# Gram-Schmidt inside an attention kernel: vectors as rows of 64 partitions instead of columns, the leading row spread by DMA

## The chip, the cores and the metric

The kernel runs on one core of a Trainium2 chip. A core has five engines that run side by side, each through its own queue of instructions in strict order: TensorE (PE in the profile, with PEld for its weight loads), VectorE (DVE), ScalarE (ACT), GpSimd (POOL) and SyncE (SP, which here only issues DMAs). They meet only at semaphores. The metric is the device time of one execution in microseconds.

## What is computed

An attention block with a bias, a feed-forward block, and a response whose matrices come from two orthonormalised 256 x 32 matrices U and V. Cut to what matters here:

```python
def gram_schmidt(X):                       # X is 256 x 32
    for i in range(32):
        q = Q[:, i]
        q = q / (norm(q) + EPS)
        Q = Q.at[:, i].set(q)
        coeffs = q @ Q[:, i + 1:]
        Q = Q.at[:, i + 1:].add(-outer(q, coeffs))
...
scores = q @ k.T / 4 + attention_bias      # 32 batches, 16 heads, 256 x 256
scores = where(src_mask, -inf, scores)
probs = softmax(scores)
x = x + (probs @ v) @ Wo + bo
x = x + gelu2(ln(x) @ W1 + b1) @ W2 + b2
...
U_o = gram_schmidt(U); V_o = gram_schmidt(V)
basis = U_o @ V_o.T
response = ((x @ basis) @ basis.T[:, :32]) @ resp_w.T + resp_b + safety_bias
out = x + strength * response
```

Gram-Schmidt has 32 steps, each dependent on the one before. There are also 32 batches, and the kernel does one step in each batch of the attention.

## The kernel before

It has two stages. The first loops over the 32 batches of the attention and stores the result x2 to DRAM; the second loops over them again for the feed-forward block and the response. `run_batches` writes out the first three and last three batches and loops over the rest, two at a time. Each engine has a `body` that is written by hand: what stands in it is what the engine does in one period, in that order, and several batches are in flight at once (the tail of batch b-1, the main part of b, the preparation of b+1).

The parts of a period that matter here, by engine:

- **PE**: `scores` (four heads at a time, L1185), `transposes` of the exponentials (one head at a time, four 128x128 transposes, L1200), `pv` (L1223), the projections, `project_o` (L1287). `transposes(b, h)` writes one of two PSUM banks, so it waits until head h-2 has been copied out of that bank. Heads 3, 7 and 11 are copied by DVE (`copy_pT`, L607), the others by ACT (L922). Head 13 therefore waits for DVE's copy of head 11.
- **DVE**: `reduce_head` (L601, two instructions of 256 columns for each head, each with a short read of its accumulator), copies out of PSUM, statistics of a later batch (`stats`, L501).
- **ACT**: the exponentials (L917) and most copies.
- **POOL**: it adds the mask to the bias of four heads at a time, `add_mask` (L430, two instructions of 1024 columns each, both operands in SBUF), makes the mask's values (L420) and normalises x (L397 to L411).
- **SP**: it loads bias, x and mask, and stores x2. The bias of half a batch is two transfers of 1 MB (L288).

A Gram-Schmidt step goes round all of them. U and V lie as columns, 128 partitions by 2 x 2 x 32 (`uv`). ACT copies out column i (`gs_column`, L938). PE multiplies it, spread over 128 columns, with all the vectors, and so gets its products with each in every partition (`gs_gram`, L1159, four matmuls of 32 columns, between `ctx_transpose` and the transposes of head 10). DVE takes the squared norm and masks the products to later vectors (`gs_products`, L577 and L579, behind head 15 and ahead of `stats` and the copy of head 11). POOL, one period on, takes the root and adds epsilon (`gs_norm`, L376 and L379), DVE inverts it (`gs_reciprocal`, L583), ACT scales (`gs_coefficients`, L943 and L944), POOL forms four outer products and adds them (`gs_update`, L386 and L389), and ACT writes the finished column back (`gs_write`, L950).

After the last batch `response_matrix` makes the matrices of the second stage from U and V.

Of the kernel before, what the change touches and what calls it, by code (L numbers as in the profile page):

```python
# [31 lines left out]
P = 128  # L32
# [81 lines left out]
def attention_block_kernel(nc, x, itok, fside, score, mask, W_ada, b_ada, Wq, bq, Wk, bk, Wv, bv, Wo, bo,  # L114
                           W1, b1, W2, b2, g2, beta2, U, V, safety_bias, gate_w1T, gate_b1, gate_w2T, gate_b2,
                           resp_wT, resp_b, freqs, out):
    with ExitStack() as ctx:
# [6 lines left out]

        x2_d = nc.dram_tensor("x2_d", (B, S, D), F32, kind="Internal").ap()
# [7 lines left out]
        ident = sb("ident", [P, P]); later = sb("later", [P, R, R]); expo = sb("expo", [P, 2, 2])  # L133
# [6 lines left out]
        uv = sb("uv", [P, 2, DC, R]); ucol = sb("ucol", [P, 2, DC]); gsb = sb("gsb", [P, 2, R]); gii = sb("gii", [P, 2])  # L140
        nrm = sb("nrm", [P, 2]); nrme = sb("nrme", [P, 2]); rnrm = sb("rnrm", [P, 2]); qcol = sb("qcol", [P, 2, DC]); gprod = sb("gprod", [P, 2, DC, R]); coef = sb("coef", [P, 2, R])
# [71 lines left out]
        gs_ps = bank[7][:, 0:2 * R].rearrange("p (a r) -> p a r", a=2)  # L213
# [4 lines left out]
        s_gcol = sem("s_gcol"); s_gram = sem("s_gram"); s_gii = sem("s_gii"); s_gnrm = sem("s_gnrm"); s_gp = sem("s_gp"); s_grec = sem("s_grec"); s_gcoef = sem("s_gcoef"); s_gprod = sem("s_gprod"); s_gupd = sem("s_gupd"); s_gself = sem("s_gself")  # L218
# [20 lines left out]
        def load_x01(sp, i):  # L239
# [5 lines left out]
                     (uv[:, 0], columns(U)), (uv[:, 1], columns(V))]  # L245
# [25 lines left out]
        def _(sp):  # L271
# [87 lines left out]
        def _(pool):  # L359

            nc.gpsimd.memset(ident[:], 0.0)
            nc.gpsimd.memset(later[:], 1.0)
# [5 lines left out]
            nc.gpsimd.affine_select(out=later[:], in_=later[:], compare_op=ALU.is_gt, fill=0.0, base=0,  # L368
                                    pattern=[[-1, R], [1, R]], channel_multiplier=0).then_inc(s_const, 1)
# [65 lines left out]
            def body(b, n):  # L435
# [52 lines left out]
        def _(dve):  # L488
# [43 lines left out]
            ins.then_inc(s_perm, 1)  # L532
            nc.vector.memset(half[:, 0:1], 0.0)
# [37 lines left out]

            def gs_products(b):
                i = b.n
                dve.wait_ge(s_gram, i + 1)
                if b.i is not None or b.off >= 1:
                    dve.wait_ge(s_gcoef, i)
                nc.vector.tensor_copy(gii[:], gs_ps[:, :, bass.ds(i, 1)].rearrange("p a r -> p (a r)"))  # L577
                ahead = later[:, bass.ds(i, 1)].to_broadcast([P, 2, R])
                nc.vector.scalar_tensor_tensor(gsb[:], gs_ps, -1.0, ahead, ALU.mult, ALU.mult).then_inc(s_gii, 1)  # L579
# [5 lines left out]
            def response_matrix():  # L585

                dve.wait_ge(s_rm, 1)
# [926 lines left out]
```

## Time and profile before

| | us |
|---|---|
| median of three runs | 1352.67 (1352.37 to 1352.85) |
| the profiled execution | 1352.78 |
| its span in the trace | 1350.6 |
| busy: PE, PEld | 1302.0, 1101.9 |
| busy: DVE, ACT, POOL | 1071.7, 1084.2, 871.8 |

The first stage takes the span up to about 885 us, the second the rest. Share of busy time is read by stage: POOL works over nine tenths of the first stage and about a quarter of the second. The time between the span and the profiled execution's own time, about 2.2 us, lies around the program.

### The profile page before, as it was taken

To read this page: it belongs to the slowest core of one execution; us is meant where nothing else is said; L and a number is where in the kernel's file an instruction comes from. 1 tells how busy PE (TensorE), PEld (TensorE's weight loads), DVE (VectorE), ACT (ScalarE), POOL (GpSimd) and SP (SyncE) were. 2 spreads that over 40 slices of the span, in tenths; PEclk is the share of its full clock that TensorE was granted. 3 is DMA by queue.
4 is the path that set the end of the run, shared out by engine and by line. 5 is a ranking of instruction groups with operands and counts; after the bars stand their busy time and mean duration, and the time that the engine had idled before them with its cause. 6 is when DMAs were issued, how large, how long until landed. Compare 5 with 4: busy or idle time off the path is not lost. (4 is left out here: it accounts for less than half of the span.)

```text
span 1350.6 us, 39501 instructions
## 1 busy us (share of the span) xinstructions
PE 1302.0 (96%) x11802; PEld 1101.9 (82%) x11802; DVE 1071.7 (79%) x3669; ACT 1084.2 (80%) x2697; POOL 871.8 (65%) x874
## 2 busy tenths in 40 slices
PE   4999999999999999999999999879999999999997
PEld 3777777777777777777777777559999999999996
DVE  4777787877778787777878778668888888888885
ACT  1788888888888888888888887867888888888873
POOL 4999989998998999899999989322222222222210
PEclk9999999999999999999999999979999999999998
DMA  9646555564655556465555674010101111111100
GB/s 288 191 146 211 174 183 181 173 210 146 211 169 186 178 175 205 150 211 166 190 174 179 203 224 133 25 32 25 47 31 47 31 46 31 39 38 34 43 25 32
DMA packets 182669, 175.05 MB, mean 130 GB/s; under 512 B 15552, under 2 KB 182112, under 8 KB 182624
## 3 DMA queue, kind: packets, MB, share of 16 engines
q1 hardware_dynamic: 181248, 173.64, 40.4%
q10 hardware_dynamic: 1376, 0.85, 0.2%
q8 instruction: 24, 0.39, 0.1%
q14 instruction: 21, 0.17, 0.0%
HBM read 157.69 MB, written 16.78 MB: 129 GB/s over the span
## 5 line engine op out<-in xcount | busy, mean ns | idle before, releaser
L430 POOL TENSOR_TENSOR ring<-ring,maskv 128x1024 f32<-128x1024 f32 x256 | 600.0, 2371 | 12.2 <-DMA ring<-in_fside 4.9
L917 ACT ACTIVATE ring<-ring,nmax 128x256 f32<-128x256 f32 x1024 | 452.6, 502 | 24.1 <-DVE nmax L601 24.1
L601 DVE CUSTOM_DVE_ANT_0 ring<-bank,ring 128x256 f32<-128x256 f32 x1024 | 373.1, 419 | 90.5 <-PE bank L1185 72.9
L922 ACT ACTIVATE pT<-bank 128x512 f32<-128x512 f32 x416 | 239.3, 592 | 102.0 <-PE bank L1200 101.9
L1200 PE MATMUL bank<-ident,ring 128*128 128x128 f32 x2048 | 292.3, 278 | 1.4 <-ACT pT L922 1.1
L1200 PEld LDWEIGHTS bank<-ident,ring 128*128 128x128 f32 x2048 | 231.7, 142 | 70.8 <-issue 47.9
L1052 ACT ACTIVATE work<-bank,b1t 128x256 f32<-128x256 f32 x256 | 107.6, 476 | 76.0 <-PE bank L1394 76.0
L1185 PE MATMUL bank<-work 32*128 32x256 f32 x2048 | 148.5, 404 | 6.0 <-DVE nmax L601 5.2
L1394 PE MATMUL bank<-hT_high,w_high 128*128 128x256 f32 x512 | 148.0, 289 | 4.3 <-DVE hT_rest L774 2.4
L1407 PE MATMUL bank<-w_high,gT_high 128*128 128x256 f32 x512 | 148.0, 289 | 0.0
L1394 PE MATMUL bank<-hT_rest,w_high 128*128 128x256 f32 x512 | 145.5, 284 | 0.0
L1407 PE MATMUL bank<-w_high,gT_rest 128*128 128x256 f32 x512 | 145.2, 284 | 0.0
L1407 PE MATMUL bank<-w_rest,gT_high 128*128 128x256 f32 x512 | 145.2, 284 | 0.0
L1394 PE MATMUL bank<-hT_high,w_rest 128*128 128x256 f32 x512 | 145.1, 283 | 0.0
L1223 PE MATMUL bank<-pT,vt 128*32 128x256 f32 x2048 | 137.0, 385 | 2.7 <-ACT pv_sb L928 1.6
L462 POOL TENSOR_SCALAR vpeb<-mvb 128x2 f32<-128x2 f32 x32 | 6.2, 194 | 201.6 <-DVE mvb L690 201.4
L1185 PEld LDWEIGHTS bank<-work 32*128 32x128 f32 x2048 | 93.4, 186 | 38.3 <-issue 27.8
L476 POOL TENSOR_TENSOR work<-work,b2b 128x512 f32<-128x512 f32 x32 | 41.7, 1302 | 126.2 <-DVE work L805 126.2
L790 DVE SCALAR_TENSOR_TENSOR pT<-work 128x512 f32<-128x512 f32 x128 | 88.6, 692 | 42.2 <-ACT work L1056 29.8
L1394 PEld LDWEIGHTS bank<-hT_high,w_high 128*128 128x128 f32 x512 | 97.8, 191 | 4.9 <-DVE hT_rest L774 2.6
L1407 PEld LDWEIGHTS bank<-w_rest,gT_high 128*128 128x128 f32 x512 | 98.5, 192 | 0.0
L1407 PEld LDWEIGHTS bank<-w_high,gT_high 128*128 128x128 f32 x512 | 98.4, 192 | 0.0
(161 smaller groups left out, 2666.8 us busy)
## 6 DMA issues: line engine op xcount, KB each, us to landing
ring<-in_fside SPq DMA_DIRECT2D x128, 1024.0 KB, 7.6
xt<-in_x SPq DMA_DIRECT2D x32, 256.0 KB, 3.1
x_d<-x2s SPq DMA_DIRECT2D x32, 256.0 KB, 7.9
work<-x_d SPq DMA_DIRECT2D x32, 256.0 KB, 2.7
out<-pT SPq DMA_DIRECT2D x32, 256.0 KB, 2.2
mk<-in_mask SPq DMA_DIRECT2D x32, 64.0 KB, 6.7
w<-in_W SPq DMA_DIRECT2D x2, 1024.0 KB, 10.5
wada<-in_W_ada SPq DMA_DIRECT2D x1, 512.0 KB, 8.1
```

Source lines behind the costliest of these rows:

```text
L430: nc.gpsimd.tensor_tensor(v, v, m, ALU.add).then_inc(s_masked, 1)
L476: nc.gpsimd.tensor_tensor(yb[:, b.par], y2[:, b.par], b2b[:].unsqueeze(1).to_broadcast([P, QT, D]), ALU.add).then_inc(s2_yb, 1)
L601: nc.vector.tensor_tensor_reduce(out=v, in0=score_ps[h % HG][:, qt], in1=v, scale=-1.0, scalar=ROW_MAX_NEG, op0=ALU.add, op1=ALU.min, accu ...
L790: nc.vector.scalar_tensor_tensor(gT[:, 2 * j:2 * j + 2], th[:, j], 1.0, up[:, j], ALU.add, ALU.mult).then_inc(s2_g, 1)
L917: nc.scalar.activation(v, v, ACT.Exp, bias=nmax[:, b.par, h, qt:qt + 1], scale=-1.0).then_inc(s_exp, 1)
L922: nc.scalar.activation(pT[:, h % (2 * HG)], tp_ps[h % 2], ACT.Copy).then_inc(s_pta, 1)
L1052: ins = nc.scalar.activation(th[:, j, f], tiles2(j)[:, f], ACT.Tanh, bias=b1t[:, 2 * j + f:2 * j + f + 1], scale=0.5 * GELU_A)
L1185: ins = mm(score_ps[r][:, qt], qm[rows, b.par, a, c, qt * P:(qt + 1) * P], kT[rows, b.par, c], start=True, stop=True)
L1200: ins = nc.tensor.transpose(tp_ps[h % 2][:, kt, qt * P:(qt + 1) * P], ring[:, slot, qt, h % CH, kt * P:(kt + 1) * P], ident[:])
L1223: ins = mm(pv_ps[VW * j:VW * (j + 1), :], vt[:, b.par, kt, h], pT[:, h % (2 * HG), kt], start=(kt == 0), stop=(kt == QT - 1))
L1394: ins = mm(tiles2(j)[:, f], w1s[kw][:, c, n * P:(n + 1) * P], hTs[kx][:, b.par, c], start=(c == 0 and k == 0), stop=(c == DC - 1 and k == ...
L1407: ins = mm(tiles2(4)[:, t], gTs[kx][:, b.par, f, t * P:(t + 1) * P], w2s[kw][:, f], start=(f == 0 and k == 0), stop=(f == FC - 1 and k == ...
```

## The change

The vectors of U and V are now kept as rows: `uvT` has 64 partitions (32 vectors of U, then 32 of V) of 256 columns. A step is done on all 64 at once.

- At the start PE transposes the columns (`vectors_transposed`) and DVE copies them to `uvT` (`gs_start`).
- In each period SP waits for the update of the step before, writes `uvT` to DRAM, waits for that, and loads row i of U and row i of V, each spread over 32 partitions, into `row`. This stands behind the mask's load and ahead of the bias transfer of batch b+2 (`vector_rows`).
- `gs_gram`, `gs_column` and `gs_write` are gone. DVE forms the products of every vector with the leading one, and its squared norm, as two sums along 256 columns (`gs_products`), with `uvT` and `row` both in SBUF.
- Which vector is earlier, leading or later is a column of a table (`roles`), that ACT copies out (`gs_role`). `gs_coefficients` is three instructions of one column, each waiting for the one before.
- POOL's `gs_norm` also scales `uvT` by a role (`uvz`), and `gs_update` is one product and one sum of 64x256. `gs_update` moves from behind `add_mask(b, 3)` to ahead of it.
- After the last batch PE transposes the rows back, and the response's matrices take one step more; DVE's copies for it stand behind its `split_weights(0)`.

```diff
+            def vector_rows(b):
+                sp.wait_ge(s_gupd, b.n + 1)
+                sp.dma_start(uv_d, uvT[:]).then_inc(s_uvst, 16)
+                sp.wait_ge(s_uvst, 16 * b.n + 16)
+                for a in range(2):
+                    sp.dma_start(row[a * R:(a + 1) * R], uv_d[bass.ds(b.n + a * R, 1)].rearrange("o d -> (o d)").partition_broadcast(R)).then_inc(s_row, 16)
...
                     load_mask(b.plus(2))
+                vector_rows(b)
                 if n is None or n + 2 < B:
                     sp.wait_ge(s_tp, H * b.n + CH)
                     load_bias(b.plus(2), 0)
...
             def gs_norm(i):
                 pool.wait_ge(s_gii, i + 1)
+                pool.wait_ge(s_grole, i + 1)
                 pool.nop(nofuse=True)
-                nc.gpsimd.tensor_tensor(nrm[:], gii[:], expo[:, 1], ALU.pow).then_inc(s_gp, 1)
+                nc.gpsimd.tensor_tensor(nrm[:], gii[:], expo[0:2 * R, 1, 0:1], ALU.pow).then_inc(s_gp, 1)
+                nc.gpsimd.tensor_scalar(uvz[:], uvT[:], role[:, 2:3], 1.0, ALU.mult, ALU.mult)
...
             def gs_update(i):
-                for a in range(2):
-                    for c in range(DC):
-                        ins = nc.gpsimd.tensor_scalar(gprod[:, a, c], coef[:, a], qcol[:, a, c:c + 1], 1.0, ALU.mult, ALU.mult)
-                ins.then_inc(s_gprod, 1)
+                nc.gpsimd.tensor_scalar(gprod[:], row[:], coef[:, 0:1], 1.0, ALU.mult, ALU.mult).then_inc(s_gprod, 1)
                 pool.wait_ge(s_gprod, i + 1)
-                nc.gpsimd.tensor_tensor(uv[:], uv[:], gprod[:], ALU.add).then_inc(s_gupd, 1)
+                nc.gpsimd.tensor_tensor(uvT[:], uvz[:], gprod[:], ALU.add).then_inc(s_gupd, 1)
...
                     add_mask(b, 2)
-                    add_mask(b, 3)
                 if step:
                     gs_update(b.plus(-1).n)
+                if main:
+                    add_mask(b, 3)
...
             def gs_products(b):
-                dve.wait_ge(s_gram, i + 1)
+                dve.wait_ge(s_row, 32 * b.n + 32)
                 if b.i is not None or b.off >= 1:
                     dve.wait_ge(s_gcoef, b.n)
-                nc.vector.tensor_copy(gii[:], gs_ps[:, :, bass.ds(i, 1)].rearrange("p a r -> p (a r)"))
-                nc.vector.scalar_tensor_tensor(gsb[:], gs_ps, -1.0, ahead, ALU.mult, ALU.mult).then_inc(s_gii, 1)
+                nc.vector.scalar_tensor_tensor(prods[:, 0], uvT[:], 1.0, row[:], ALU.mult, ALU.mult, accum_out=dot[:])
+                nc.vector.scalar_tensor_tensor(prods[:, 1], row[:], 1.0, row[:], ALU.mult, ALU.mult, accum_out=gii[:]).then_inc(s_gii, 1)
...
             def gs_coefficients(i):
+                act.wait_ge(s_gii, i + 1)
+                act.wait_ge(s_grole, i + 1)
+                nc.scalar.activation(dotm[:], dot[:], ACT.Copy, scale=role[:, 0:1]).then_inc(s_gdot, 1)
                 act.wait_ge(s_grec, i + 1)
+                act.wait_ge(s_gdot, i + 1)
+                nc.scalar.activation(share[:], dotm[:], ACT.Identity, bias=role[:, 1:2], scale=rnrm[:, 0:1]).then_inc(s_gshare, 1)
+                act.wait_ge(s_gshare, i + 1)
+                nc.scalar.activation(coef[:], share[:], ACT.Copy, scale=rnrm[:, 0:1]).then_inc(s_gcoef, 1)
...
                 if main:
-                    gs_gram(b, n)
                     transposes(b, 10)
                     transposes(b, 11)
```

Where this stands in the engines' queues, taken from a batch that is written out. On DVE, at the end of a batch's heads, before (`gii` and `gsb` are the squared norm and the masked products, `pT` takes the copy of head 11, L601 is the reduction of a head):

```order
L601 ISA ring,nmax<-bank,ring 128x256
L601 ISA nmax 128x1
L577 COPY gii<-bank 128x2
L579 SCALAR_TENSOR_TENSOR gsb<-bank,later 128x64
L501 BN_STATS st<-xt 128x6 x2
L607 COPY pT<-bank 128x512
```

and of the change (L622 is the reduction now, L628 the copy of head 11):

```order
L622 ISA ring,nmax<-bank,ring 128x256
L622 ISA nmax 128x1
L596 SCALAR_TENSOR_TENSOR prods,dot<-uvT,row 64x256
L597 SCALAR_TENSOR_TENSOR prods,gii<-row 64x256
L512 BN_STATS st<-xt 128x6 x2
L628 COPY pT<-bank 128x512
```

Two instructions on PSUM are replaced by two of 256 columns whose inputs both lie in SBUF, still ahead of the copy of head 11.

On POOL, from one step's norm to the next batch's first mask additions, before (`ring` is the bias):

```order
L376 TENSOR_TENSOR nrm<-gii,expo 128x2
L379 TENSOR_SCALAR nrme<-nrm 128x2
L430 TENSOR_TENSOR ring<-ring,maskv 128x1024 x4
L386 TENSOR_SCALAR gprod<-coef,qcol 128x32 x4
L389 TENSOR_TENSOR uv<-uv,gprod 128x128
L420 TENSOR_SCALAR maskv<-mk 128x512
L430 TENSOR_TENSOR ring<-ring,maskv 128x1024 x2
L397 TENSOR_SCALAR vpe<-mv 128x2
```

and of the change (L440 is the mask addition now):

```order
L388 TENSOR_TENSOR nrm<-gii,expo 64x1
L389 TENSOR_SCALAR uvz<-uvT,role 64x256
L392 TENSOR_SCALAR nrme<-nrm 64x1
L440 TENSOR_TENSOR ring<-ring,maskv 128x1024 x2
L397 TENSOR_SCALAR gprod<-row,coef 64x256
L399 TENSOR_TENSOR uvT<-uvz,gprod 64x256
L440 TENSOR_TENSOR ring<-ring,maskv 128x1024 x2
L430 TENSOR_SCALAR maskv<-mk 128x512
L440 TENSOR_TENSOR ring<-ring,maskv 128x1024 x2
L407 TENSOR_SCALAR vpe<-mv 128x2
```

The update now has two mask additions more behind it and two fewer ahead of it.

## Rows read from the trace of the kernel before

**Rows 1.** Busy by stretch: us from:to, length, engines (instructions), PE clock, DMA.

```profile
400.00:500.00 100.00, 100.00 (x960) 77.14 (x962) 79.11 (x330) 85.43 (x214) 91.22 (x86) 1.00 0.57 183
```

**Rows 2.** Timeline of PE: start, length, line, operation, count [idle before].

```profile
417.08 1.15 PE L1185 MATMUL bank<-work 32*128 32x256 f32 x16
...
419.09 0.98 PE L1159 MATMUL bank<-uv,ucol 128*128 128x32 f32 x8
...
419.90 1.07 PE L1200 MATMUL bank<-ident,ring 128*128 128x128 f32 x8
...
421.91 1.15 PE L1185 MATMUL bank<-work 32*128 32x256 f32 x16
...
422.98 1.09 PE L1200 MATMUL bank<-ident,ring 128*128 128x128 f32 x8
```

**Rows 3.** Timeline of DVE, same period, and one reciprocal earlier.

```profile
404.88 0.16 DVE L583 RECIPROCAL rnrm<-nrme 128x2 f32<-128x2 f32 x1
...
418.50 0.43 DVE L601 CUSTOM_DVE_ANT_0 ring<-bank,ring 128x256 f32<-128x256 f32 x1 [0.99 <-PE bank L1185]
...
421.26 0.15 DVE L577 COPY gii<-bank 128x2 f32 x1
...
421.46 0.74 DVE L501 BATCH_NORM_STATS2 st<-xt 128x6 f32<-128x256 f32 x2
...
422.12 0.67 DVE L607 COPY pT<-bank 128x512 f32<-128x512 f32 x1
```

**Rows 4.** Timeline of ACT: the last of the four coefficient instructions.

```profile
410.32 0.31 ACT L944 ACTIVATE coef<-gsb,rnrm 128x32 f32<-128x32 f32 x1
```

**Rows 5.** Timeline of POOL over one period.

```profile
410.81 1.08 POOL L386 TENSOR_SCALAR gprod<-coef,qcol 128x32 f32<-128x32 f32 x4 [1.10 <-ACT coef L944]
411.96 0.46 POOL L389 TENSOR_TENSOR uv<-uv,gprod 128x128 f32<-128x128 f32 x1
...
413.30 4.69 POOL L430 TENSOR_TENSOR ring<-ring,maskv 128x1024 f32<-128x1024 f32 x2 [0.17 <-POOL maskv L420]
...
419.81 1.10 POOL L411 TENSOR_SCALAR xn<-xt,rstd,nmr 128x256 f32<-128x256 f32 x2 [0.21 <-POOL nmr L402]
...
425.51 0.72 POOL L376 TENSOR_TENSOR nrm<-gii,expo 128x2 f32<-128x2 f32 x1
...
426.67 9.35 POOL L430 TENSOR_TENSOR ring<-ring,maskv 128x1024 f32<-128x1024 f32 x4
437.10 1.07 POOL L386 TENSOR_SCALAR gprod<-coef,qcol 128x32 f32<-128x32 f32 x4 [1.08 <-ACT coef L944]
```

**Rows 6.** Timeline of DVE and POOL where both read SBUF at once.

```profile
841.90 2.59 DVE L675 TENSOR_TENSOR cb<-cb 128x256 f32<-128x256 f32 x1
...
902.45 0.68 DVE L798 TENSOR_TENSOR gT_rest<-pT,gT_high 128x512 fp32r<-128x512 f32 x1
903.05 1.75 DVE L774 TENSOR_TENSOR hT_rest<-work,hT_high 128x512 fp32r<-128x512 f32 x1
```

**Rows 7.** The same place on POOL.

```profile
902.54 1.71 POOL L476 TENSOR_TENSOR work<-work,b2b 128x512 f32<-128x512 f32 x1
```

**Rows 8.** One line's instructions: count, shortest/median/longest ns, first and last start.

```profile
L469 POOL TENSOR_TENSOR nmrb<-mnegb,rstdb x32: 196/672/737, 884.3 to 1296.0; 128x2 f32<-128x2 f32 x32
```

**Rows 9.** DMA issues: tensors, queue, count, KB each, median us to landing.

```profile
xt<-in_x SPq DMA_DIRECT2D x32, 256.0 KB, 3.1
x_d<-x2s SPq DMA_DIRECT2D x32, 256.0 KB, 7.9
```

**Rows 10.** Timeline of SP: the bias transfer behind the new place.

```profile
415.16 1.00 SPq L288 DMA_DIRECT2D ring<-in_fside  x2
```

**Rows 11.** Timeline of PE after idle times of two lengths.

```profile
865.00 1.07 PE L1223 MATMUL bank<-pT,vt 128*32 128x256 f32 x16 [1.17 <-DVE ctxn L649]
...
904.86 0.46 PE L1394 MATMUL bank<-hT_high,w_high 128*128 128x256 f32 x1 [2.37 <-DVE hT_rest L774]
```

**Rows 12.** Busy by stretch behind the second of them.

```profile
904.90:908.30 3.40, 3.40 (x16) 3.40 (x17) 3.19 (x6) 2.08 (x6) 0.00 (x0) 0.52 0.33 82
```

More of the change, by code:

```diff
@@ L361, in _ @@
             nc.gpsimd.memset(ident[:], 0.0)
-            nc.gpsimd.memset(later[:], 1.0)
+            nc.gpsimd.memset(tri[:], -1.0)
             nc.gpsimd.memset(expo[:, 0], -0.5)
@@ L367, in _ @@
                                     pattern=[[-1, P]], channel_multiplier=1)
-            nc.gpsimd.affine_select(out=later[:], in_=later[:], compare_op=ALU.is_gt, fill=0.0, base=0,
-                                    pattern=[[-1, R], [1, R]], channel_multiplier=0).then_inc(s_const, 1)
+            nc.gpsimd.affine_select(out=tri[:], in_=tri[:], compare_op=ALU.is_gt, fill=0.0, base=0,
+                                    pattern=[[-1, 2 * R]], channel_multiplier=1).then_inc(s_const, 1)
             pool.wait_ge(s_const, 1)
@@ L532, in _ @@
             ins.then_inc(s_perm, 1)
+            for a in range(2):
+                rows = slice(a * R, (a + 1) * R)
+                nc.vector.tensor_copy(roles[rows, 0], tri[rows, a * R:(a + 1) * R])
+                nc.vector.tensor_copy(roles[rows, 1], ident[rows, a * R:(a + 1) * R])
+                link(nc.vector.tensor_scalar(roles[rows, 2], ident[rows, a * R:(a + 1) * R], -1.0, 1.0, ALU.mult, ALU.add))
             nc.vector.memset(half[:, 0:1], 0.0)
@@ L757, in body @@
                 if n == B:
-                    response_matrix()
+                    response_matrix(0)
                     split_weights(0)
+                    response_matrix(1)
             reduces(first, (0, 1, 2))
+            gs_start()
             v_out(first)
@@ L1007, in body @@
                 if main:
-                    gs_column(b.n)
+                    gs_role(b.n)
                     copy_pT(b, 8)
@@ L1148, in bias_rows, with vectors_transposed @@
                 mm(bank[6][:, 0:2 * DC], perm[:], bqr[:].rearrange("p t c -> p (t c)"), start=True, stop=True).then_inc(s_bqk, 1)
-            def gs_gram(b, n):
-                pe.wait_ge(s_gcol, b.n + 1)
-                if n is None or n + 1 < B:
-                    pe.wait_ge(s_v, b.n + 2)
-                if n is None or n >= 1:
-                    pe.wait_ge(s_gself, b.n)
-                for a in range(2):
-                    for c in range(DC):
-                        ins = mm(gs_ps[:, a], ucol[:, a, c:c + 1].to_broadcast([P, P]), uv[:, a, c], start=(c == 0), stop=(c == DC - 1))
-                ins.then_inc(s_gram, 1)
+            def vectors_transposed():
+                for c in range(DC):
+                    ins = nc.tensor.transpose(bank[6][0:2 * R, c * P:(c + 1) * P], uv[:, c].rearrange("p a r -> p (a r)"), ident[:])
+                ins.then_inc(s_uvt, 1)
             def response_matrix(step):
                 if step == 0:
-                    pe.wait_ge(s_gself, R)
+                    pe.wait_ge(s_gupd, R + 1)
                     pe.wait_ge(s_reduced, 2 * H * B)
                     for c in range(DC):
-                        mm(bank[0][0:R, 0:R], uv[:, 1, c], uv[:, 1, c], start=(c == 0), stop=(c == DC - 1))
-                    ins = mm(bank[1][0:R, 0:D], uv[0:R, 0, 0], respT[:], start=True, stop=True)
+                        ins = nc.tensor.transpose(bank[2][:, 2 * R * c:2 * R * (c + 1)], uvT[:, c * P:(c + 1) * P], ident[0:2 * R, 0:2 * R])
                 if step == 1:
                     pe.wait_ge(s_rmc, 1)
+                    for c in range(DC):
+                        mm(bank[0][0:R, 0:R], uv[:, c, 1], uv[:, c, 1], start=(c == 0), stop=(c == DC - 1))
+                    ins = mm(bank[1][0:R, 0:D], uv[0:R, 0, 0], respT[:], start=True, stop=True)
+                if step == 2:
+                    pe.wait_ge(s_rmc, 2)
                     ins = mm(t_ps, gram[:].rearrange("p k r -> p (k r)"), t1[:], start=True, stop=True)
@@ L1209, in pv @@
                         pe.wait_ge(s_ctxn, 2 * b.n)
+                    else:
+                        pe.wait_ge(s_gupd, 1)
                 if g == 1:
@@ L1297, in _ @@
             pe.wait_ge(s_load_att, 16 * len(loads_att))
+            vectors_transposed()
             project_v(first)
-            x_back(first, False)
+            x_back(first)
             def y_transpose(b):
@@ L1366, in body @@
                     response_matrix(1)
+                    response_matrix(2)
                 if main:
```

60 lines of the change are left out of this document (25 added, 35 removed).

## The prediction, made before the change was run

> **What bounds the kernel now.** I read the slices and the busy times by stretch first: in the first stage PE is never idle and its clock is full, with POOL at 91% and ACT and DVE below that [rows 1]. Then PE's timeline: each group of matmuls begins about when the one before it ends, so a period is the sum of PE's work [rows 2]. The period is the distance between two updates on POOL, 437.10 - 410.81 = 26.29 us [rows 5]. The second stage is bound by PE too, and the change doesn't touch its loop. So the question is what happens to the 26.29 us in each of some 30 periods. The span lies 2.2 us under the execution's own time of 1352.78; the sum is made against 1352.78, which is 0.1 above the median.
>
> **What the change removes.** PE loses `gs_gram`: it starts at 419.09, and the next transposes at 419.90 [rows 2], so 0.81 us a period of the engine that sets the period, or 31 x 0.81 = 25 us in all if nothing else becomes late. ACT trades four coefficient instructions and a column's write for three chained ones of one column. The last of the four ends at 410.32 + 0.31 = 410.63 [rows 4], and I leave the end of the coefficients there; a few tenths either way do nothing below but shift POOL.
>
> **What it adds on DVE, and why that is on the path.** PE's transposes of head 13 wait for DVE's copy of head 11, since both use one PSUM bank. Heads 12 and 13 are the eight matmuls from 422.98; the second four begin half of 0.91 us later, at 423.44. DVE's copy ends at 422.12 + 0.67 = 422.79 [rows 3]. So the copy may come 0.65 us later before PE notices it at today's period. It can't come earlier: it stands behind the eight reductions from 418.50 [rows 3], and those stand behind PE's scores at 417.08 [rows 2], which are ahead of the removed matmuls. That makes a new loop: scores of heads 12 to 15, reductions, products, statistics, copy of head 11, transposes of head 13, the rest of PE's period. Its length is 26.29 + (delay of the copy - 0.65). Against it, PE's own work is 25.48.
>
> The copy is delayed by what the two products take over the 0.20 us that `gs_products` takes now (421.26 to 421.46, [rows 3]). The eight reductions ahead of them have 256 columns and an accumulator's read too, and take 421.26 - 418.50 = 2.76, which is 0.345 each from start to start [rows 3]. An undisturbed sum of 512 columns takes 0.68 [rows 6], so the products can't cost much more. I take 0.35 to 0.40 each; alone the pair takes 0.75, and the delay is 0.55: just inside the 0.65.
>
> **But they are not alone.** Both inputs of each product are in SBUF, and POOL's mask additions read SBUF nine tenths of the time. The trace has that meeting in other places. At 902.45 DVE runs such an instruction, POOL's addition issued at 902.54 takes 1.71 us until 904.25, and DVE's next, issued at 903.05, takes 1.75 us instead of 0.68: it stood until POOL was done [rows 6, 7]. So one waits for the other in full, and of two DVE instructions in a row the second is overtaken by POOL's waiting one. In the first stage itself the one sum of 256 columns of two SBUF tensors took 2.59 us, one mask addition longer than it should [rows 6]. In the second stage POOL's product of two columns takes 196 ns alone but 672 in the median, beside DVE's SBUF work [rows 8]. None of DVE's instructions in a period of the first stage has two SBUF inputs today: scores, copies and additions read one input from PSUM.
>
> The Trainium skill states this as a rule ("SBUF — State Buffer", section "Who interferes with whom"): a DVE instruction with two SBUF inputs and a GpSimd instruction that reads SBUF exclude each other, and the one that came second blocks until the first has ended. By that rule the change costs what the next part works out; without it the pair costs 0.75 us and the change about nothing. The rows on tensors of 128 partitions agree with it; none shows 64.
>
> **Which POOL instruction the products meet.** POOL's order decides, and the change moves it. The update begins 0.18 us behind the coefficients, at 410.81 [rows 4, 5]. Its product of 256 columns costs 0.55 (half of the 1.10 for two of that size), its sum 0.73: between 0.46 for 128 columns and 2.34 (4.69 / 2) for 1024, by the line through both [rows 5]. With gaps it ends at about 412.2. Then the two mask additions that used to be ahead of it, 4.69, to 416.95; the mask's values with the gaps around them, 413.30 - 411.96 - 0.46 = 0.88, to 417.8; the next batch's first two additions, 4.69, to 422.4 or 422.5 [rows 5]. DVE's products are due at 421.26 [rows 3]: inside the second addition, which runs from about 420.1. The first product then waits 1.15 us, to 422.4, and takes some 0.35. Next on POOL stands a small instruction (`vpe`, about 0.2), then the second product, 0.35. The statistics start at 423.3 instead of 421.46, a delay of 1.85, and the loop is longer by 1.85 - 0.65 = 1.2 us; with the coefficients 0.1 to 0.2 us earlier it is 1.05. I take **1.15 us a period**.
>
> **POOL keeps up.** Its period holds 1.1 us of waiting for the coefficients [rows 5], so 25.2 of work. It gains the scaling of `uvT` (0.55 and a gap), and the update changes from 1.54 to 1.28; that makes 25.6, and some tenths of waiting for DVE, under 27.4. Today it waits behind all four groups of masks, tomorrow behind three, so it runs a group later against DVE: the norm comes at about 422.5 + (425.51 - 413.30 - 4.69) = 430.0 in place of 425.51 and is done by 431.8, with the scaling between [rows 5]. DVE asks for it at 404.88 + 26.29 + 1.15 = 432.3 [rows 3]. The heads 12 to 15 get their mask at 416.95, DVE needs it at 418.50. Thin, but it fits.
>
> **SP and the transfers.** `uvT` goes out at 412.2, and the rows are needed at 421.26: 9 us for two transfers in a row. A transfer in a quiet queue lands in 3.1 us (x), one behind bias loads in 7.9 (x2) [rows 9]; here the bias of the next batch has been under way since 401 and is in, so I take 3.1 each, and with 1 us for issuing the rows are there by 419.5. The bias transfer of batch b+2, now issued at 415.16 [rows 10], goes out a little later, at about 416; POOL reads it a period on, so this costs nothing. The extra traffic is 64 KB out and 64 KB in a period, next to 2 MB of bias.
>
> **Ends of the program.** In the last two batches POOL has no more masks to add, so nothing meets; there the kernel gains a few tenths. The transposes and copies at the start and the longer `response_matrix` cost a few tenths each. I take +0.5 in all. Sum: 1352.78 + 30 x 1.15 + 0.5 = 1387.8, so **1388 us**. The case's own range is 1371 to 1403: a first product that waits 0.6 to 1.65 us.
>
> **Rivals.**
>
> *A. The products don't wait* (64 partitions, or this form, might not exclude POOL). Then the delay is 0.55 against 0.65, the loop is 26.19, and with the ends the time is 1352.78 - 30 x 0.1 + 0.5 = 1350. This is the side on which the change is not slower: it is faster once the pair costs under 0.83, and the most it could give, with free products, is 0.65 a period or 1333. For it: no row shows 64 partitions. Against: every row with two SBUF inputs beside POOL shows the wait.
>
> *B. POOL is later by over 1.2 us*, so that the products fall into the first of the two additions. The first product waits for its end, POOL takes its second addition, and the second product waits for all of it: 2.2 to 3.4 us a period, 1419 to 1455. For it: a slower update or late coefficients move POOL that way. Against: 1.2 us is as much as the whole update is priced at.
>
> *C. PE's clock falls in the new gap.* PE would be ready for head 13 at 422.6 to 423 and starts at 424.6, idle for 1.6 to 1.9 us. After 1.17 us idle matmuls ran on at full speed; after 2.37 us one took 0.46 [rows 11], and the granted clock of the 3.4 us behind it was 0.52, nearly all of it at the lower level of 1.2 GHz [rows 12]. The gap lies between. Half speed for 3.4 us costs 1.7: 30 x 2.85 + 0.5 gives 1439. With B it is 1470 to 1506.
>
> *D. The rows come late.* At 7.9 us for each transfer they come at 429, 7.8 us behind the products' place: over 200 us more. For it: the same queue carries the bias; against: the order of the issues.
>
> **How the numbers follow.** The forecast's case gets 0.60, A 0.12, B 0.12, C 0.10, D 0.06. Something under 0.2% (2.7 us) can't be told from no change. A lies at that bound, so I give faster 0.04, same 0.09; slower 0.87. The range that leaves out A, D and the upper part of B is **1358 to 1456**: it takes in a first product that hardly waits, and the clock's case.
>
> **What would show it.** Right: two products on DVE of which the first takes about 1.5 us and the second 0.6; PE idle ahead of a transpose group, released by DVE's copy of head 11; a period of 27.4 on POOL, whose wait for the coefficients is still there, about 1.5 us long. A: products of 0.4 us and a period of 26.2. B: a second product of 2.5 us or more. C: a granted clock under 1.00 in the first stage. D: DVE waiting for `row`. The forecast is wrong at its root if the copy of head 11 isn't what PE waits for.

## The result, and the profile after the change

| | before | after |
|---|---|---|
| median of four runs, us | 1352.76 (1352.37 to 1354.17) | 1390.80 (1385.48 to 1391.91) |
| the profiled execution, us | 1352.78 | 1385.48 |
| its span, us | 1350.6 | 1383.7 |

The changed kernel is slower: 1.0272 times the time before, 95% interval 1.0244 to 1.0299. The forecast was 1388. A second set of runs of the same kernel, `r_after` below, gave 1388.05 and 1.0265 (1.0244 to 1.0286), so I take the two together: 35 to 38 us more. Two of the ten executions of `b1_one_input` below (1376.01 and 7208.93 us) fell in a slower state of the chip and are left out of its figures; every other execution used here is a fast one.

First the two lines of the page after that say most: the busy times, and PE's transposes with the idle time ahead of them and what ended it.

```profile
PE 1288.7 (93%) x11550; PEld 1076.5 (78%) x11550; DVE 1120.6 (81%) x3741; ACT 1082.3 (78%) x2633; POOL 872.8 (63%) x810
...
L1215 PE MATMUL bank<-ident,ring 128*128 128x128 f32 x2048 | 300.9, 279 | 43.5 <-DVE pT L628 42.7
```

PE is busy 13 us less than before (1302.0). The matmuls that went (L1159) were busy for 31.3 us, in part overlapping their neighbours, and the transposes, in shorter groups now, are busy for 300.9 us instead of 292.3. PE stands idle for 42.7 us until DVE's copies into `pT` (L628) are done. The same kernel's busy times by stretch (length, engines, PE clock, DMA) show it in the steady state; before, PE was busy for all of these 100 us [rows 1].

```profile
400.00:500.00 100.00, 93.72 (x888) 70.73 (x889) 80.81 (x324) 82.20 (x197) 89.15 (x77) 1.00 0.57 177
```

PE's timeline of the changed kernel, around the end of one period and at the same place a period earlier (start, length, idle time before in brackets); it answers to [rows 2].

```profile
410.56 0.65 PE L1215 MATMUL bank<-ident,ring 128*128 128x128 f32 x4 [1.45 <-DVE pT L628]
...
430.51 1.15 PE L1200 MATMUL bank<-work 32*128 32x256 f32 x16
...
434.82 1.15 PE L1200 MATMUL bank<-work 32*128 32x256 f32 x16
435.90 0.66 PE L1215 MATMUL bank<-ident,ring 128*128 128x128 f32 x4
438.00 0.65 PE L1215 MATMUL bank<-ident,ring 128*128 128x128 f32 x4 [1.45 <-DVE pT L628]
```

The transposes of heads 12 and 13 used to run as one group of eight. Now head 12 runs at 435.90, PE then waits 1.45 us, and head 13 runs when the copy of head 11 has left its bank. The distance of two such waits is the new period: 438.00 - 410.56 = 27.44 us, against 26.29 before. 26 periods in a row have this wait, each 1.44 to 1.47 long.

What holds the copy back is on DVE, beside POOL (timelines of the changed kernel, same period; they answer to [rows 3] and [rows 5]):

```profile
434.68 0.08 DVE L622 DVE_READ_ACCUMULATOR2_ANT nmax<- 128x1 f32 x1
434.68 1.58 DVE L596 SCALAR_TENSOR_TENSOR prods<-uvT,row 64x256 f32<-64x256 f32 x1
...
436.19 0.41 DVE L597 SCALAR_TENSOR_TENSOR prods<-row 64x256 f32<-64x256 f32 x1
...
436.54 0.74 DVE L512 BATCH_NORM_STATS2 st<-xt 128x6 f32<-128x256 f32 x2
437.20 0.67 DVE L628 COPY pT<-bank 128x512 f32<-128x512 f32 x1
```

```profile
424.43 0.47 POOL L397 TENSOR_SCALAR gprod<-row,coef 64x256 f32<-64x256 f32 x1 [2.18 <-ACT coef L970]
424.98 0.72 POOL L399 TENSOR_TENSOR uvT<-uvz,gprod 64x256 f32<-64x256 f32 x1
425.67 4.67 POOL L440 TENSOR_TENSOR ring<-ring,maskv 128x1024 f32<-128x1024 f32 x2
...
431.29 4.68 POOL L440 TENSOR_TENSOR ring<-ring,maskv 128x1024 f32<-128x1024 f32 x2 [0.17 <-POOL maskv L430]
436.07 0.24 POOL L407 TENSOR_SCALAR vpe<-mv 128x2 f32<-128x2 f32 x1
```

The first product is issued at 434.68, inside POOL's mask addition, and ends at 436.26, 0.29 after the addition's end (435.97). The second stands beside POOL's short `vpe` and takes 0.41. In the last batch POOL has no masks left, and there the first product takes 0.41 too:

```profile
904.73 0.41 DVE L596 SCALAR_TENSOR_TENSOR prods<-uvT,row 64x256 f32<-64x256 f32 x1
```

### The profile page after: what moved, and what is told of

Its sections match the earlier page's. It is cut to its first block and busy times, and to the rows that moved or that the text cites. A ratio compares the mean times of both kernels' runs of the same rounds, so it can differ in the third digit from the quotient of the medians.

```text
span 1383.7 us, 39096 instructions
## 1 busy us (share of the span) xinstructions
PE 1288.7 (93%) x11550; PEld 1076.5 (78%) x11550; DVE 1120.6 (81%) x3741; ACT 1082.3 (78%) x2633; POOL 872.8 (63%) x810
## 5 line engine op out<-in xcount | busy, mean ns | idle before, releaser
L440 POOL TENSOR_TENSOR ring<-ring,maskv 128x1024 f32<-128x1024 f32 x256 | 601.0, 2369 | 12.1 <-DMA ring<-in_fside 4.7
L622 DVE CUSTOM_DVE_ANT_0 ring<-bank,ring 128x256 f32<-128x256 f32 x1024 | 372.2, 415 | 71.5 <-PE bank L1200 70.2
L945 ACT ACTIVATE pT<-bank 128x512 f32<-128x512 f32 x416 | 243.2, 593 | 133.1 <-PE bank L1215 131.3
L1215 PE MATMUL bank<-ident,ring 128*128 128x128 f32 x2048 | 300.9, 279 | 43.5 <-DVE pT L628 42.7
L813 DVE SCALAR_TENSOR_TENSOR pT<-work 128x512 f32<-128x512 f32 x128 | 88.6, 692 | 42.7 <-ACT work L1073 30.1
L1423 PEld LDWEIGHTS bank<-w_high,gT_rest 128*128 128x128 f32 x512 | 98.7, 193 | 0.0
```

Of the source, the lines that this page charges most:

```text
L440: nc.gpsimd.tensor_tensor(v, v, m, ALU.add).then_inc(s_masked, 1)
L622: nc.vector.tensor_tensor_reduce(out=v, in0=score_ps[h % HG][:, qt], in1=v, scale=-1.0, scalar=ROW_MAX_NEG, op0=ALU.add, op1=ALU.min, accu ...
L813: nc.vector.scalar_tensor_tensor(gT[:, 2 * j:2 * j + 2], th[:, j], 1.0, up[:, j], ALU.add, ALU.mult).then_inc(s2_g, 1)
L945: nc.scalar.activation(pT[:, h % (2 * HG)], tp_ps[h % 2], ACT.Copy).then_inc(s_pta, 1)
L1215: ins = nc.tensor.transpose(tp_ps[h % 2][:, kt, qt * P:(qt + 1) * P], ring[:, slot, qt, h % CH, kt * P:(kt + 1) * P], ident[:])
L1423: ins = mm(tiles2(4)[:, t], gTs[kx][:, b.par, f, t * P:(t + 1) * P], w2s[kw][:, f], start=(f == 0 and k == 0), stop=(f == FC - 1 and k == ...
```

## Experiments

The theory has two halves. **The loop**: DVE's copy of head 11 has a little slack, and what comes ahead of it beyond this slack lengthens the period. **The exclusion**: a DVE instruction whose two inputs are in SBUF and a POOL instruction that reads SBUF wait for each other. The main rivals are that products of this size cost what they cost anyway, and that the period is longer for another reason (the three chained coefficient instructions, POOL's order, the rows' transfers). Each experiment changes one thing.

### The same instructions with one input each

`e1_one_input` is the changed kernel, in which each product becomes a maximum of one tensor. The products are left out, so the vectors are not orthogonalised; all else is there.

```diff
-                nc.vector.scalar_tensor_tensor(prods[:, 0], uvT[:], 1.0, row[:], ALU.mult, ALU.mult, accum_out=dot[:])
-                nc.vector.scalar_tensor_tensor(prods[:, 1], row[:], 1.0, row[:], ALU.mult, ALU.mult, accum_out=gii[:]).then_inc(s_gii, 1)
+                nc.vector.tensor_reduce(dot[:], uvT[:], mybir.AxisListType.X, ALU.max)
+                nc.vector.tensor_reduce(gii[:], row[:], mybir.AxisListType.X, ALU.max).then_inc(s_gii, 1)
```

> The changed kernel with DVE's two products replaced by two maxima along the same 256 columns, one of uvT and one of row, so that each instruction has one input in SBUF instead of two (left out: the products; the vectors come out wrong). Everything else stays: the DMAs, the wait for row, POOL's order. Theory (two SBUF inputs wait for POOL's mask additions): the pair takes 0.7 to 0.8 us in place of 1.9, the copy of head 11 comes some 0.5 us later than before the change, which its slack of 0.65 covers; period 26.2 us, 1349 to 1354. Rival (the length of the DVE stretch, the row's DMAs or ACT's chain make the loss): it stays at 1385 to 1391.

Measured: 1351.17 us (1348.04 to 1356.23), 0.9985 of the kernel before (0.9971 to 0.9999). The ten executions form two groups: five at a mean granted clock of 0.991 took 1348.0 to 1350.6, five at 0.987 took 1351.7 to 1356.2. Neither is near 1388. Timelines of DVE and PE in `e1_one_input`:

```profile
418.51 0.41 DVE L596 TENSOR_REDUCE dot<-uvT 64x1 f32<-64x256 f32 x1
418.85 0.40 DVE L597 TENSOR_REDUCE gii<-row 64x1 f32<-64x256 f32 x1
...
420.63 0.65 PE L1215 MATMUL bank<-ident,ring 128*128 128x128 f32 x4 [0.24 <-DVE pT L628]
```

Each of the pair costs 0.34 from start to start, although POOL runs a mask addition beside them, and PE's wait shrinks from 1.45 to 0.24. The loss goes with the second SBUF input. The operation was changed as well (a maximum for a product with a sum), but a product alone takes the same 0.41, as the last batch above shows; a product with one input in SBUF and one in PSUM was not run. What is left is a kernel that ties with the one before, although PE has 25 us less to do: the loop through the copy is then as long as the old period (26.23).

### The same test on the kernel before

Here nothing of the change is present; one, or four, spare instructions of 64x256 stand behind `gs_products(b)`, ahead of the statistics and the copy of head 11.

`b1_one_input` and `b4_one_input` (one line, or four like it):

```diff
                     gs_products(b)
+                    nc.vector.tensor_reduce(spsum[:, 0:1], bob[0:2 * R], mybir.AxisListType.X, ALU.max)
```

> The kernel before the change, with one DVE instruction added behind its gs_products: a maximum along 256 columns of 64 partitions, one SBUF input. Theory (the copy of head 11 has 0.65 us of slack against PE): it takes 0.35 us, inside the slack, and the time stays within 2 us of the kernel before. Rival (PE waits for DVE already, any work there is paid): 30 x 0.35 = 10 us more.

Measured: 1353.3 us (the median of eight, 1352.37 to 1354.65) against 1352.98, 1.0002 (0.9992 to 1.0013). Nothing: 0.33 us fits in the slack, and the period in its trace is 26.29 as before.

> The same with four such instructions, one SBUF input each, 1.4 us in all. Theory: 1.4 - 0.65 = 0.75 us a period over 30 periods, 22 us more than the kernel before (18 to 26). Rival without the slack: 42 more; rival in which this place is not on the path: none.

Measured: 1376.23 us (1374.72 to 1377.31) against 1352.98, ratio 1.0168 (1.0151 to 1.0185). DVE and PE in `b4_one_input`:

```profile
406.19 0.40 DVE L753 TENSOR_REDUCE spsum<-bob 64x1 f32<-64x256 f32 x1
...
408.95 0.65 PE L1205 MATMUL bank<-ident,ring 128*128 128x128 f32 x4 [0.58 <-DVE pT L608]
```

Four of them delay the copy by 4 x 0.33 = 1.31, and the kernel is 23.3 us longer, 0.78 in each of 30 periods. So the slack is 1.31 - 0.78 = 0.53 us. (By the periods of the two traces, 27.09 and 26.29, it is 0.51.)

`b1_two_inputs`:

```diff
                     gs_products(b)
+                    nc.vector.scalar_tensor_tensor(spare[:], bob[0:2 * R], 1.0, bvb[0:2 * R], ALU.mult, ALU.mult, accum_out=spsum[:, 0:1])
```

> The kernel before the change, with one DVE product added behind its gs_products: 64 partitions by 256 columns of two constant SBUF tensors, with an accumulator. It differs from the run with one added maximum only in its second SBUF input. Theory: at that place (421.5 in the trace of before) POOL runs the first of two mask additions (420.9 to 423.2), so the product waits 1.75 us and ends 2.1 later; 2.1 - 0.65 = 1.45 a period, 43 us more than the kernel before (35 to 50). Rival (two inputs on 64 partitions cost nothing by themselves): as with the one maximum, no more than 2 us.

Measured: 1398.49 us (1397.06 to 1399.18) against 1352.98, 1.0332 (1.0315 to 1.0349). DVE, POOL and PE in `b1_two_inputs`:

```profile
415.24 2.04 DVE L753 SCALAR_TENSOR_TENSOR spare<-bob,bvb 64x256 f32<-64x256 f32 x1
...
414.62 4.87 POOL L431 TENSOR_TENSOR ring<-ring,maskv 128x1024 f32<-128x1024 f32 x2
...
418.67 0.65 PE L1202 MATMUL bank<-ident,ring 128*128 128x128 f32 x4 [1.25 <-DVE pT L608]
```

One instruction with two SBUF inputs costs 45.5 us, one of the same size with one input costs nothing that can be measured. It was issued 0.62 us into POOL's pair of additions and had to wait for the first of them. This also shows both halves of the theory without any of the change's DMAs, coefficients or order on POOL.

### Nothing ahead of the copy

`e4_no_products` replaces the two products by two `memset` (`dot` is 0, `gii` is 1), which leaves the sums out. `e2_behind_copy` keeps them and moves `gs_products(b)` behind the copy:

```diff
                     reduces(b, (12, 13, 14, 15))
-                    gs_products(b)
                     if n is None or n + 3 < B:
                         stats(b.plus(3))
                     copy_pT(b, 11)
+                    gs_products(b)
```

> The changed kernel with the two products replaced by two memsets of 64x1 (left out: the products; the coefficients are constants). DMAs, waits, ACT's and POOL's parts stay. Theory: the copy of head 11 comes at the time of before the change or 0.1 us earlier, so of PE's 0.81 us some 0.65 to 0.8 can be had: period 25.5 to 25.65, 1331 to 1335. Rival (POOL or ACT bind first, at 25.9 or more): 1341 and above. If the row's DMAs were the loss: 1385 and above.

Measured: 1339.84 us (1337.82 to 1341.39), 0.9888 (0.9867 to 0.9910), period 25.8.

> The changed kernel with the two products moved behind the copy of head 11 (order: statistics, copy of head 11, products). Theory: PE no longer waits for that copy; the products are due when POOL's second mask addition has just ended and meet its small instructions, so both together take 0.8 to 1.0 us; DVE reaches the next batch's reductions 0.2 us later than before the change and is level or up to 0.4 ahead at the x2 sum; period 25.6 to 25.9, 1332 to 1342, faster than before the change, because PE's 0.81 us are now worth something. Rival (the contention costs DVE the same wherever the products stand): period 26.5 or more, 1360 and above.

Measured: 1345.25 us (1343.19 to 1345.62), 0.9928 (0.9908 to 0.9948), with periods of 25.80 and 26.09 in turn. Both gains are under 2%, but the intervals leave 1 out: both are faster than the kernel before, and both less so than expected (1331 to 1335 and 1332 to 1342). DVE in `e2_behind_copy`:

```profile
420.14 0.40 DVE L596 SCALAR_TENSOR_TENSOR prods<-uvT,row 64x256 f32<-64x256 f32 x1
420.49 0.41 DVE L597 SCALAR_TENSOR_TENSOR prods<-row 64x256 f32<-64x256 f32 x1
...
403.17 0.15 DVE L601 RECIPROCAL rnrm<-nrme 64x1 f32<-64x1 f32 x1 [0.70 <-POOL nrme L392]
```

Behind the copy the products meet POOL's short instructions and take 0.4 each. A new wait has come up: DVE's reciprocal stands 0.70 us for POOL's norm (0.62 in `e4_no_products`), and what is behind it on DVE is late by that. How much of it reaches PE, the next run shows. The prediction had called this margin thin, 0.5 us at a period of 27.4; at 26 it is gone.

`e7_late_reciprocal` is `e2_behind_copy` with `gs_reciprocal` moved back too, behind the reductions of three heads and DVE's copy of head 3:

```diff
                 if main:
                     reduce_head(b, 4)
-                if tail:
-                    gs_reciprocal(b.plus(-1).n)
                 if main:
                     reduces(b, (5, 6, 7))
                     copy_pT(b, 3)
+                if tail:
+                    gs_reciprocal(b.plus(-1).n)
```

> The changed kernel with the products behind the copy of head 11, and besides with DVE's reciprocal moved from between heads 4 and 5 to behind the copy of head 3. With the products moved alone, DVE waited 0.6 to 0.7 us in front of the reciprocal for POOL's norm, and PE lost 0.3 us at the transposes of heads 4 and 5; ACT needs the reciprocal only some 4 us later. Theory: that wait goes and the period falls from 26.1 to 25.8, 7 to 10 us less, 1336 to 1339. Rival (PE's 0.3 us come from something else, or POOL's 25.3 us of work and its waits bind): no change, 1343 to 1346.

Measured: 1340.53 us (1338.91 to 1340.81), 0.9905 (0.9888 to 0.9921). The busy times by stretch, and DVE's timeline at the reciprocal, of `e7_late_reciprocal`:

```profile
400.00:500.00 100.00, 99.53 (x944) 75.83 (x938) 82.63 (x348) 86.58 (x211) 93.88 (x80) 1.00 0.62 192
```

```profile
404.54 0.14 DVE L601 RECIPROCAL rnrm<-nrme 64x1 f32<-64x1 f32 x1
```

The wait is gone and PE is busy 99.5 of 100 us, at a period of 25.78. The time is again a little above the 1336 to 1339 expected. The step from `e2_behind_copy` is small: the two ratios' intervals overlap, and only the traces (25.94 on average and 25.78 a period, about 5 us in 30) separate the two. Of the versions run that compute all that the reference asks for this is the fastest: 12.5 us less than the kernel before, 48 to 50 less than the changed one, by two DVE steps moved. `e4_no_products`, which leaves the sums out, has about the same time.

Of PE's saving of 0.81 a period only 0.51 comes through (26.29 - 25.78), because a second loop binds. `scores` of the next batch's first heads waits until DVE has reduced heads 12 to 15. In the changed kernel DVE's last read for them ends at 434.76 and PE's scores start at 434.82; before the change DVE was done at about 421.3 and PE came only at 421.91 [rows 2]. Without `gs_gram` PE would be there 0.81 earlier, at 421.10, and has to wait. The start of the scores in `e7_late_reciprocal` shows this as 0.16 us, and there is another 0.13 just ahead of it, at the transposes of heads 10 and 11, whose cause was not looked for.

### Where the products meet POOL

If the exclusion is right, the price depends on POOL's phase. `e3_update_last` puts `gs_update` back behind `add_mask(b, 3)`, which starts POOL's last pair of additions later against DVE. `p1_pool_later` and `p3b_pool_later` delay POOL by one and three spare instructions behind the update:

```diff
                 nc.gpsimd.tensor_tensor(uvT[:], uvz[:], gprod[:], ALU.add).then_inc(s_gupd, 1)
+                nc.gpsimd.tensor_scalar(spare[:], bob[0:2 * R], 1.0, 1.0, ALU.mult, ALU.mult)
```

> The changed kernel with POOL's update moved back behind the fourth group of mask additions, as it was before the change. Theory (POOL's phase decides what the products meet): behind the update now stand the mask values, two additions and the normalising, so that at the products' place the two additions of the next group (from about 9.8 us behind the coefficients) are running: the first product waits for the end of the first, 1.5 us, POOL's second addition overtakes, and the second product waits 2.4 us; the copy comes 4.4 us later than before the change, a period of 30 us at full clock (1465), and about 1.7 more if PE's clock falls in a gap of over 3 us (1516). Rival (the wait is an average of POOL's load, whatever its phase): as the changed kernel, 1385 to 1391.

Measured: 1532.29 us (1528.63 to 1534.26), 1.1304 (1.1280 to 1.1329). DVE, POOL and PE in `e3_update_last`:

```profile
409.25 2.10 DVE L595 SCALAR_TENSOR_TENSOR prods<-uvT,row 64x256 f32<-64x256 f32 x1
...
411.29 2.54 DVE L596 SCALAR_TENSOR_TENSOR prods<-row 64x256 f32<-64x256 f32 x1
...
408.71 4.85 POOL L440 TENSOR_TENSOR ring<-ring,maskv 128x1024 f32<-128x1024 f32 x2
...
415.23 1.11 PE L1214 MATMUL bank<-ident,ring 128*128 128x128 f32 x4 [4.11 <-DVE pT L627]
416.13 3.62 PE L1301 MATMUL bank<-wo,ctxT 128*128 128x256 f32 x8
```

The first product waits for the addition that is running, and the second for the whole of the next one: 2.10 and 2.54. PE stands for 4.11 us and then runs at half speed (0.65 becomes 1.11, and 1.89 becomes 3.62). The periods are 31.79 and 33.06 in turn. The 30 us expected at full clock, with 1.7 for a fall of the clock, are the shorter ones; the longer ones were not expected, and so the time lies above the 1516 given as the worst. The update's new place, which looks like an unrelated detail of the change, spares it 140 us.

> The changed kernel with one more instruction on POOL behind the update: a scaling of 64x256 into a spare tensor, 0.47 us as uvz. POOL itself has 2.2 us of waiting a period, so it can take it. Theory (the first product waits for the end of POOL's second mask addition): that end comes 0.55 us later, the product takes 2.1 instead of 1.58, and the period is 0.55 longer: 16 us more than the changed kernel, 1400 to 1408. Rival (DVE's wait does not hang on POOL's phase): no change, 1385 to 1391.

Measured: 1419.02 us (1410.12 to 1419.75), 1.0462 (1.0425 to 1.0499). DVE and PE in `p1_pool_later`:

```profile
257.42 1.98 DVE L597 SCALAR_TENSOR_TENSOR prods<-uvT,row 64x256 f32<-64x256 f32 x1
...
233.30 0.65 PE L1216 MATMUL bank<-ident,ring 128*128 128x128 f32 x4 [1.85 <-DVE pT L629]
```

and its busy times in the 4 us behind this wait and behind the next one, which is as long (PE's clock is the last value but two):

```profile
233.30:237.30 4.00, 4.00 (x32) 3.48 (x36) 3.24 (x15) 2.27 (x5) 4.00 (x4) 1.00 0.29 66
261.00:265.00 4.00, 3.86 (x14) 3.08 (x15) 2.07 (x13) 1.39 (x3) 3.92 (x4) 0.62 0.20 66
```

The spare instruction takes 0.40 us, the first product 0.40 more (1.98 for 1.58), PE's wait 0.40 more (1.85 for 1.45), and the period is 27.84, also 0.40 more. The waits add one for one, as expected, though each by 0.40 and not 0.55. What was not expected is the clock: behind about every third or fourth of these waits it falls (0.62 over 4 us), and that period is 29.52, 1.7 longer. It is 31 us above `r_after`, not the 12 to 20 expected. In the 25 periods between the waits at 120.24 and 828.10 the trace holds 7 such long periods; these 25 are together 21.7 us longer than in `r_after`, which is 25 x 0.40 + 7 x 1.7. Ahead of them the kernel is 11 us later already: there one wait is 3.87 us long, and the clock fell three times.

> The changed kernel with three more instructions on POOL behind the update, scalings of 64x256 into spare tensors. They make POOL 1.6 us later, past the 1.05 us at which the products' place falls into the first of the two mask additions. Theory: the first product waits about 0.6 us for the end of that addition, POOL's second addition goes ahead, and the second product waits 2.3 us; the pair takes 3.3 us instead of 2.0, 1.3 to 1.7 us a period: 1425 to 1442 with PE at full clock. PE then stands for 2.8 to 3.2 us a period, and if its clock falls in each, 1.7 us a period more: 1475 to 1495. The run with one such instruction, whose gaps of 1.85 us were followed by a longer period about one time in three, makes the second more likely. Rival (no threshold, POOL's lateness adds as it is): one long product of 3.1 us and one of 0.4.

Measured: 1455.24 us (1452.03 to 1456.81), 1.0742 (1.0724 to 1.0759), between the two values expected. DVE, POOL and PE in `p3b_pool_later`:

```profile
441.68 0.41 DVE L599 SCALAR_TENSOR_TENSOR prods<-uvT,row 64x256 f32<-64x256 f32 x1
...
442.03 2.56 DVE L600 SCALAR_TENSOR_TENSOR prods<-row 64x256 f32<-64x256 f32 x1
...
439.42 4.90 POOL L443 TENSOR_TENSOR ring<-ring,maskv 128x1024 f32<-128x1024 f32 x2 [0.17 <-POOL maskv L433]
...
476.10 0.65 PE L1218 MATMUL bank<-ident,ring 128*128 128x128 f32 x4 [2.44 <-DVE pT L631]
```

The first product slips in at the border between POOL's two additions and costs nothing, where 0.6 us of waiting were expected; the second waits for all of the second addition, 2.56. This is rival B of the prediction, brought about by delaying POOL. Periods are 28.43 where the clock stays, one in three, and 30.10 where it falls.

### The changed kernel again

`r_after` is the changed kernel unedited.

> The changed kernel itself once more. Its first profiled execution took 1385.5 us and the timed ones 1390 to 1392; this shows what its spread is. No theory distinguishes the two.

Measured: 1388.05 us (1385.69 to 1392.55), ratio 1.0265. Its profile has the same waits of 1.45 us. In both sets the profiled execution is the fastest, 1385.5 and 1385.7, and others take up to 7 us more. The traces can't show where these are, since only the profiled executions have one. Falls of the clock explain at most a part: one fall costs 1.7 us and would lower the mean granted clock by about 0.001, but the three others of the first set, 5 to 6 us longer, were granted 0.988, 0.988 and 0.989 against 0.988 in the profiled one. Only the longest of the second set had less, 0.986. The rest stays open.

## Why the prediction was right

The time, 1390.8 and 1388.1 in the two sets, lies within 3 us of the forecast of 1388, and each part of its mechanism was seen.

- **The loop through the copy of head 11.** Right: PE's idle time is released by that copy, `b1_one_input` and `b4_one_input` show the slack, and `e2_behind_copy` removes the loss by moving the products past it. The slack was mis-sized: 0.65 predicted, 0.53 by `b4_one_input`. The estimate let the copy end at the moment at which PE starts; the trace of after has 0.13 us between the two (437.20 + 0.67 = 437.87, and 438.00).
- **The exclusion.** Right, and now shown at 64 partitions by `e1_one_input` and by `b1_two_inputs` against `b1_one_input`. The Trainium skill's rule ("SBUF — State Buffer", section "Who interferes with whom") agrees with these runs; rival A, that the rule would not hold here, falls. The description of the chip ahead of the prediction, that the engines meet only at semaphores, is too simple: DVE and POOL also meet in SBUF, and there one instruction took 2.04 us instead of 0.4.
- **The phase.** Right within 0.1 us: the first product was to take 1.5 and took 1.58. With the wait taken out (1.58 - 0.41 = 1.17) it is the 1.15 that the prediction worked out from POOL's order.
- **The second product.** Off: 0.2 us was added for `vpe`, which POOL starts ahead of it. The products start 434.68 and 436.19, the statistics 436.54: 1.51 + 0.35 = 1.86 over the pair, a delay of 1.86 - 0.20 = 1.66 in place of 1.85. The short instruction cost nothing.
- **The sum.** The two sizes that were off have opposite signs: 1.66 - 0.53 = 1.13 a period. Measured is 27.44 - 26.29 = 1.15, the term of the forecast. So part of the agreement is luck: with the true delay and the slack as predicted it would have been 1.01 and the forecast 4 us lower.
- **The ends.** Predicted +0.5 on 30 equal periods, 35.0 in all. The two traces' spans differ by 33.1 us. After the first periods the changed kernel is 0.4 ahead. Its trace lacks a fall of the clock that the trace of before has, to half from 34.6 to 38.0 us; `e2_behind_copy`, which starts with the same instructions, has it too, so it is no effect of the change. The 26 full waits then give 29.9, and the two periods behind them, with waits of 1.37 and 0.69, another 1.1 and 0.3. The last 2.2 are the ends: 1.0 is idle time ahead of the scores that follow `constants2` (4.62 to 5.11 us) and at the stages' boundary (3.09 to 3.57), the rest was not traced to single waits. So the periods were counted 3.2 us too high and the ends 1.3 too low.
- **PE's saving.** Partly wrong, at no cost to the forecast. "PE's own work is 25.48" leaves out the loop from the scores through DVE's reductions to the next scores, which holds PE at 25.8 (`e4_no_products`, `e7_late_reciprocal`). So the 1333 that free products were to give was out of reach; `e4_no_products` took 1340. The 1333 doesn't follow from the prediction's own terms either: free products would also save the 0.20 of today's `gs_products`, and PE's 25.48 would bind, at 1329.
- **POOL.** It waits 2.18 us for the coefficients, not 1.5, since its work is shorter, 27.44 - 2.18 = 25.3 against the predicted 25.6, and since the tenths that it was to wait for DVE hardly came (its two short instructions beside the second product take 0.24 and 0.28 instead of 0.19). The rows below (ACT, POOL and DVE of the changed kernel) show that ACT's chain ends at 424.25, which is 10.43 us ahead of the products, where the prediction had 421.26 - 410.63 = 10.63. `gprod` takes 0.47 (0.55 predicted) and the sum 0.72 (0.73). So the late chain and the short product nearly cancel, and the addition ends 1.29 us after the products' start instead of 1.15. The norm is ready at 444.73 + 0.18 = 444.91 and DVE asks at 445.76, so the margin called thin holds here; in `e2_behind_copy` and `e4_no_products`, at a shorter period, it doesn't.

```profile
423.96 0.29 ACT L970 ACTIVATE coef<-share,rnrm 64x1 f32<-64x1 f32 x1
...
444.73 0.18 POOL L392 TENSOR_SCALAR nrme<-nrm 64x1 f32<-64x1 f32 x1
...
445.76 0.15 DVE L601 RECIPROCAL rnrm<-nrme 64x1 f32<-64x1 f32 x1
```

- **The transfers.** Mis-sized, to no effect. The page of the changed kernel has, for the DMA issues (count, KB each, us to landing),

```profile
uv_d<-uvT SPq DMA_DIRECT2D x32, 64.0 KB, 1.9
row<-uv_d SPq DMA_DIRECT2D x64, 32.0 KB, 1.8
```

where 3.1 was taken for each. DVE never waits for `row`: rival D falls.
- **Rival C, the clock.** It didn't fall in the changed kernel: 1.00 through the first stage, behind 26 gaps of 1.45 us. But the prediction had put the gap at 1.6 to 1.9 us. It is shorter because PE reaches the gap 0.3 us later than the saving of 0.81 would have it, held by DVE's reductions and by the delay ahead of them. `p1_pool_later` shows what a gap of the predicted size does: at 1.85 us the clock fell in 8 of 26 periods. That C stayed away, with a chance of 0.10, is therefore in part luck.

For the parts of the change beside the products, `e1_one_input` bounds the sum of all: with the exclusion out of the way, the chained coefficients, POOL's order, the transfers and the copy's delay together come to 0.9985 of the time before.

## What to carry to other kernels

Before DVE gets a two-input instruction on SBUF, look at what POOL does at that moment: beside a long SBUF instruction of POOL it waits for its end, and the second of two in a row can wait for POOL's whole next instruction; beside POOL's short ones (0.2 to 0.3 us) it cost its own 0.35 us here. Then look at what stands behind it on DVE that another engine waits for, and work out the slack of that one thing. The cure may be to move a few instructions and not to give up the change: with the same work in another order the kernel here went from 2.7% slower to 1% faster than before.

## What the runs showed of the hardware

- Two DVE instructions in a row, each with two SBUF inputs, don't get in together: POOL's next instruction goes between them. One mask addition (about 2.35 us) then shows as a DVE instruction of 2.54 or 2.56 us that alone takes 0.41.
- PE's clock behind idle time that returns in every period: after 1.45 us it stayed at 1.00 in 26 of 26 periods (`after`, and the same in `r_after`); after 1.85 us it fell in 8 of 26 (`p1_pool_later`); after 2.44 us in 17 of 26 (`p3b_pool_later`); after 4.11 us in all (`e3_update_last`). A single gap of 1.70 us in `after` was followed by full clock. A wait of the same length on the same work did and didn't lower it, so rows of single waits, as in [rows 11] and [rows 12], give no safe limit between 1.17 and 2.37.
- A fall costs 1.7 us in this kernel (29.52 - 27.84 and 30.10 - 28.43) behind gaps of 1.85 and 2.44 us. So the 0.40 us of delay in `p1_pool_later` costs 31.0 / 30 = 1.03 us in each period, the first batches included.
